# Selective scan: where GpSimd's seven drives take their B from

## What is computed

```python
xc = silu(conv(x_in) + conv_b)
sel = einsum('ble,se->bls', xc, sel_w)
Bm, Cm = sel[..., R:R+N], sel[..., R+N:]
dt = softplus(einsum('blr,er->ble', sel[..., :R], dt_w) + dt_b)
dA = exp(dt[..., None] * A)
dBu = dt[..., None] * Bm[:, :, None, :] * xc[..., None]
h = dA_t * h + dBu_t                    # the scan over t
y = einsum('ben,bn->be', h, C_t)        # summed over the 16 states
y = (y + D_param * xc) * silu(z)
```

## Time and profile before

| | us |
|---|---|
| median of 3 runs (1496.01 to 1501.19) | 1496.17 |
| the profiled execution | 1499.47 |
| its span, first to last instruction | 1497.7 |
| scan stage of the first pair, first scan's start to last GpSimd product's end (81.13 to 194.15) | 113.0 |
| busy in the span: PE, DVE, ACT, POOL | 1282.9, 1013.5, 592.0, 471.3 |

### The profile page before, as it was taken

How to read it: one execution, slowest core, us unless ns; L and a number is a source line. 1 busy time by engine, 2 the same in 40 slices (tenths; PEclk the granted TensorE clock), 3 DMA queues, 4 the chain that set the end, 5 groups by cost and what they waited for, 6 DMA issues and landing times.

```text
span 1497.7 us, 16634 instructions
## 1 busy us (share of the span) xinstructions
PE 1282.9 (86%) x5914; PEld 551.0 (37%) x5930; DVE 1013.5 (68%) x1106; ACT 592.0 (40%) x815; POOL 471.3 (31%) x254
## 2 busy tenths in 40 slices
PE   6957789989985789998997678999899687899988
PEld 2312333337422233334742223332573232333366
DVE  2589865575558895567555988556746599755683
ACT  0353443325344334333525433532451644343245
POOL 3259810012006990002200798000210199600030
PEclk9979999999997999999999899999999889999998
DMA  8234420000013442000001343200000134220000
GB/s 248 97 129 150 145 82 18 1 1 1 15 38 107 155 154 64 8 1 1 2 15 46 125 153 129 72 1 1 1 1 15 60 139 156 102 54 1 1 2 15
DMA packets 43378, 93.65 MB, mean 63 GB/s; under 512 B 6786, under 2 KB 23970, under 8 KB 42786
## 3 DMA queue, kind: packets, MB, share of 16 engines
q1 hardware_dynamic: 42690, 88.25, 17.8%
q10 hardware_dynamic: 608, 4.34, 1.0%
HBM read 87.84 MB, written 4.73 MB: 62 GB/s over the span
## 4 chain that ended last, share of the span: by engine, by line
PE 56%; DVE 14%; POOL 10%; ACT 8%; issue 7%; DMA 3%; SPq 1%; POOLq 0%; DVEq 0%; ACTq 0%
PE ps L654 8%; PE ps L667 8%; PE ps L675 7%; POOL scratch L456 6%; DVE scratch L1160 6%; PE ps L606 5%; PE ps L537 4%; PE ps L523 4%; DVE scratch L1149 3%; PE ps L770 2%; DVE scratch L1196 2%; PE ps L584 2%; PE ps L822 2%; PE ps L550 2%; DMA scratch<-c_rows 2%
## 5 line engine op out<-in xcount | busy, mean ns | idle before, releaser
L456 POOL TENSOR_TENSOR scratch<-scratch 128x1024 f32<-128x1024 f32 x124 | 291.2, 2367 | 340.1 <-DVE scratch L1160 340.0
L606 PE MATMUL ps<-scratch,consts 128*128 128x512 f32 x512 | 257.8, 637 | 15.4 <-POOL scratch L456 15.2
L470 POOL TENSOR_TENSOR scratch<-scratch,rmax 128x1024 f32<-128x1024 f32 x32 | 61.5, 1923 | 594.1 <-DVE rmax L1267 594.1
L1160 DVE TENSOR_TENSOR_SCAN scratch<-ps,scratch 128x1024 f32<-128x1024 f32 x100 | 225.5, 2278 | 0.5
L933 ACT ACTIVATE ps<-steps,vec 128x1024 f32<-128x1024 f32 x128 | 143.0, 1117 | 197.8 <-DVE scratch L1160 195.9
L1196 DVE TENSOR_TENSOR scratch<-scratch,ps 128x1024 f32<-128x1024 f32 x108 | 131.8, 1221 | 129.1 <-PE ps L667 122.6
L584 PE MATMUL ps<-bc,pick 128*128 128x512 bf16 x240 | 83.3, 427 | 125.4 <-DVE scratch L1149 80.7
L979 ACT ACTIVATE scratch<-ps 128x1024 f32<-128x1024 f32 x108 | 108.8, 1022 | 182.2 <-PE ps L654 182.2
L606 PEld LDWEIGHTS ps<-scratch,consts 128*128 128x128 f32 x512 | 101.9, 204 | 136.3 <-issue 92.8
L1149 DVE TENSOR_TENSOR scratch<-steps,ps 128x1024 f32<-128x1024 f32 x100 | 122.1, 1221 | 38.2 <-PE ps L584 31.9
L654 PE MATMUL ps<-h_odd,w 64*128 64x512 f32 x512 | 142.1, 641 | 3.8 <-ACT scratch L979 3.8
(11 more groups left out here) (197 smaller groups left out, 1590.0 us busy)
## 6 DMA issues: line engine op xcount, KB each, us to landing
scratch<-c_rows SPq DMA_DIRECT2D x128, 512.0 KB, 3.7
steps<-routed_table SPq DMA_DIRECT2D x128, 64.5 KB, 1.9
decayT<-in_decayT SPq DMA_DIRECT2D x8, 512.0 KB, 17.5
work<-in_table ACTq DMA_DIRECT2D x1, 2064.0 KB, 13.7
routed_table<-work SPq DMA_DIRECT2D x1, 2064.0 KB, 8.3
w<-in_w ACTq DMA_DIRECT2D x4, 512.0 KB, 20.2
out<-h_even SPq DMA_DIRECT2D x4, 512.0 KB, 2.6
bc<-in_x_next SPq DMA_DIRECT2D x3, 512.0 KB, 3.6
```

The costliest lines, as they stand in the source:

```text
L456: pool.tensor_tensor(hc_slot(k), hs_slot(k), c_slot(k), ALU.mult).then_inc(sem["hc_ready"], 1)
L606: m = mm(ps[:, 6 + c, :], ident, hc_slot(k)[:, c * CH:(c + 1) * CH], start=(n == 0), stop=(n == NS - 1))
L1160: dve.tensor_tensor_scan(hs_slot(k), banks(dA_bank(k)), dbu_slot(k), 0.0, ALU.mult, ALU.add).then_inc(sem["scanned"], 1)
```

## The change

For the seven GpSimd drives B no longer goes through TensorE, banks 0 and 1 and ScalarE. The DRAM tensor gets all 32 rows of B and C (`bc_rows`), so the two stores are twice as large, and SyncE reads B's row broadcast over the partitions into `b_sb`, ahead of the C row of step j-1, once the scan of the drive before has read `b_sb`. `copy_b`, `B_ORDER` and the seven spreads are gone; `DVE_DRIVES` lists the 25 steps that are left, and TensorE spreads the next of them at each of these steps. GpSimd's drive of step j moves from behind product j-4 to behind product j-3. The arithmetic is that of before, but that these seven steps take fp32 B in place of the sum of its three bf16 parts.

```diff
--- before.py
+++ after.py
@@ -45,9 +45,7 @@
 U_LATE = (7, 8, 11, 12)
 
 POOL_DRIVES = (5, 9, 13, 17, 21, 25, 29)
-B_ORDER = list(range(2 * NS))
-for _j in POOL_DRIVES:
-    B_ORDER[_j - 1:_j + 1] = [_j, _j - 1]
+DVE_DRIVES = [k for k in range(2 * NS) if k not in POOL_DRIVES]
 C_RING = 3
 
 Y_GATED = (NS + 8, NS + 11)
@@ -67,7 +65,7 @@
 
     xin_ps=NC, z_ps=NC, z_ready=2 * NC, xc_ready=2 * NC, sel_ps=2, dt_ps=2, sel_hi=2, sel_read=2, sel_split=1 + NC,
     dt_read=2, dt_exp=2, dt_ln=2, dt_ready=1, dt_late=NN, mid_late=1, u_ready=1, u_late=NN,
-    b_ps=2 * NS, dA_ready=2 * NS, dbu_ready=2 * NS - len(POOL_DRIVES), b_copied=len(POOL_DRIVES),
+    b_ps=2 * NS - len(POOL_DRIVES), dA_ready=2 * NS, dbu_ready=2 * NS - len(POOL_DRIVES), b_loaded=16 * len(POOL_DRIVES),
     dbu_pool=len(POOL_DRIVES), scanned=2 * NS, hc_ready=2 * NS - 1, hc_last=NC,
     c_rows=2, c_stored=16 * 2, c_loaded0=16 * 11, c_loaded1=16 * 11, c_loaded2=16 * 10,
     y_summed=2 * NS + 1, y_copied=1, gated_first=NC, gated_y=NC,
@@ -143,7 +141,7 @@
         av_bd = sb("av_bd", [P, P])
         fiT = sb("fiT", [P, 2, HID])
 
-        c_dram = nc.dram_tensor("c_rows", (2, NS, T), F32, kind="Internal").ap()
+        c_dram = nc.dram_tensor("bc_rows", (2, 2 * NS, T), F32, kind="Internal").ap()
         table_dram = nc.dram_tensor("routed_table", (P, LAYERS, NX, WCOL), F32, kind="Internal").ap()
         consts = sb("consts", [P, i["consts"].shape[1]])
         pick = sb("pick", [P, 2 * NS], BF16)
@@ -351,18 +349,25 @@
             sp.dma_start(table_dram, table).then_inc(sem["stored"], 16)
             def move(pair, more):
                 sp.wait_ge(sem["c_rows"], at(pair, "c_rows", 1))
-                sp.dma_start(c_dram[0], c_rows(0)[NS:2 * NS]).then_inc(sem["c_stored"], 16)
+                sp.dma_start(c_dram[0], c_rows(0)).then_inc(sem["c_stored"], 16)
                 sp.wait_ge(sem["c_stored"], at(pair, "c_stored", 16))
                 for k in range(2 * NS):
                     g, n = divmod(k, NS)
                     if k == C_RING:
                         sp.wait_ge(sem["c_rows"], at(pair, "c_rows", 2))
-                        sp.dma_start(c_dram[1], c_rows(1)[NS:2 * NS]).then_inc(sem["c_stored"], 16)
+                        sp.dma_start(c_dram[1], c_rows(1)).then_inc(sem["c_stored"], 16)
                     if k == NS:
                         sp.wait_ge(sem["c_stored"], at(pair, "c_stored", 32))
+                    if k + 1 in POOL_DRIVES:
+
+                        n_ = POOL_DRIVES.index(k + 1)
+                        if n_:
+                            sp.wait_ge(sem["scanned"], at(pair, "scanned", POOL_DRIVES[n_ - 1] + 1))
+                        g_, row = divmod(k + 1, NS)
+                        sp.dma_start(b_sb, c_dram[g_, row].partition_broadcast(P)).then_inc(sem["b_loaded"], 16)
                     if k >= C_RING:
                         sp.wait_ge(sem["hc_ready"], at(pair, "hc_ready", k - C_RING + 1))
-                    sp.dma_start(c_slot(k), c_dram[g, n].partition_broadcast(P))\
+                    sp.dma_start(c_slot(k), c_dram[g, NS + n].partition_broadcast(P))\
                       .then_inc(sem[f"c_loaded{k % C_RING}"], 16)
                 sp.wait_ge(sem["h_ready"], at(pair, "h_ready", NN))
                 sp.wait_ge(sem["stored"], 16)
@@ -454,13 +459,13 @@
                     if k >= 4:
                         pool.wait_ge(sem["y_summed"], at(pair, "y_summed", k - 3))
                     pool.tensor_tensor(hc_slot(k), hs_slot(k), c_slot(k), ALU.mult).then_inc(sem["hc_ready"], 1)
-                    if k + 4 in POOL_DRIVES:
-                        j = k + 4
+                    if k + 3 in POOL_DRIVES:
+                        j = k + 3
                         pool.wait_ge(sem["u_ready"], at(pair, "u_ready", 1))
                         if j >= NS:
                             pool.wait_ge(sem["u_late"], at(pair, "u_late", NN))
                         n_ = POOL_DRIVES.index(j) + 1
-                        pool.wait_ge(sem["b_copied"], at(pair, "b_copied", n_))
+                        pool.wait_ge(sem["b_loaded"], at(pair, "b_loaded", 16 * n_))
                         pool.tensor_tensor(b_sb, u[:, j // NS, :], b_sb, ALU.mult).then_inc(sem["dbu_pool"], 1)
 
                 for m in range(NM):
@@ -570,16 +575,13 @@
 
 
                 def spread_b(i):
-                    k = B_ORDER[i]
+
+                    k = DVE_DRIVES[i]
                     g, n = divmod(k, NS)
                     pe.wait_ge(sem["sel_split"], at(pair, "sel_split", 1 + NC * g))
                     pe.wait_ge(sem["dt_read"], at(pair, "dt_read", 1))
                     if i:
-                        last = B_ORDER[i - 1]
-                        if last in POOL_DRIVES:
-                            pe.wait_ge(sem["b_copied"], at(pair, "b_copied", POOL_DRIVES.index(last) + 1))
-                        else:
-                            pe.wait_ge(sem["dbu_ready"], at(pair, "dbu_ready", drives_up_to(last)))
+                        pe.wait_ge(sem["dbu_ready"], at(pair, "dbu_ready", i))
                     for c in range(NC):
                         m = mm(ps[:, c, :], pick[:, n:n + 1].to_broadcast([P, P]),
                                bc[:, g, c * CH:(c + 1) * CH], start=True, stop=True)
@@ -611,11 +613,8 @@
                 spread_b(0)
                 spread_b(1)
                 for k in range(2 * NS + LAG):
-                    if k + 2 in POOL_DRIVES:
-                        spread_b(k + 1)
-                        spread_b(k + 2)
-                    elif k and k + 1 < 2 * NS and k + 1 not in POOL_DRIVES:
-                        spread_b(k + 1)
+                    if k in DVE_DRIVES[1:-1]:
+                        spread_b(DVE_DRIVES.index(k) + 1)
                     if k == 2 * NS:
 
                         pe.wait_ge(sem["dbu_ready"], at(pair, "dbu_ready", PER["dbu_ready"]))
@@ -933,16 +932,6 @@
                     act.activation(banks(dA_bank(k)), dt[:, k // NS, :], ACT.Exp, scale=v("A", k % NS))\
                        .then_inc(sem["dA_ready"], 1)
 
-                def copy_b(j):
-                    act.wait_ge(sem["b_ps"], at(pair, "b_ps", B_ORDER.index(j) + 1))
-                    n_ = POOL_DRIVES.index(j)
-                    if n_:
-                        act.wait_ge(sem["scanned"], at(pair, "scanned", POOL_DRIVES[n_ - 1] + 1))
-                    else:
-                        act.wait_ge(sem["c_stored"], at(pair, "c_stored", 16))
-                    act.activation(b_sb, banks(0), ACT.Copy).then_inc(sem["b_copied"], 1)
-
-
                 first_parts(0)
                 dt_above(0)
                 dt_size(0)
@@ -967,8 +956,6 @@
                         act.wait_ge(sem["y_summed"], at(pair, "y_summed", NS))
                         act.wait_ge(sem["c_stored"], at(pair, "c_stored", 32))
                         act.activation(y_sum, banks(6), ACT.Copy).then_inc(sem["y_copied"], 1)
-                    if k + 2 in POOL_DRIVES:
-                        copy_b(k + 2)
                 norm(0)
 
 
@@ -1141,7 +1128,7 @@
                 def drive(k):
                     if k in POOL_DRIVES:
                         return
-                    dve.wait_ge(sem["b_ps"], at(pair, "b_ps", B_ORDER.index(k) + 1))
+                    dve.wait_ge(sem["b_ps"], at(pair, "b_ps", drives_up_to(k)))
                     if k >= 2:
                         dve.wait_ge(sem["scanned"], at(pair, "scanned", k - 1))
                     if k == NS:
```

## The result

The changed kernel took 1515.76 us (median of 1508.62, 1513.13, 1518.39 and 1522.39), the kernel before, run beside it, 1497.85. The ratio is 1.0117, 95% interval 1.0075 to 1.0159: slower by 17.9 us. The forecast was 1485.2, faster, with a range to 1495.

What follows compares the result with a forecast made beforehand. In the scan stage VectorE and GpSimd were taken as both nearly full, VectorE waiting 31.9 us for B's spreads. A gain of 23.0 less 12.0 for late B rows, 11.0 us, took 1496.17 to 1485.2; range 1473 to 1495.

Steps and rivals of the forecast that it cites:

- VectorE up to S(6): VectorE in the first pair: step 6's scan ends 26.32 us after step 0's scan starts.
- S(0): S(k) is step k's scan on VectorE; this is step 0's, from whose start each pair's times are counted.
- the cover of y's copy: ScalarE's copy of y and decay 19 end at 149.3, before step 19's scan is due at 149.9: covered by 0.6.
- where B is late: Drives 13, 17, 21, 25 and 29, where GpSimd runs without a gap, wait for B; 5 and 9 do not.
- GpSimd's work: GpSimd from step 6's product to step 30's, with drives 9 to 29: 80.5 us if it never waits.
- H(30): H(k) is step k's product on GpSimd; this is step 30's.
- how late B's row is: B lands 5.2 us after step j-5's product, asked for at 4.6: 0.6 late, twenty times, 12 us.
- the fourth case: Rival: B rows queue behind two C rows, 1.9 late, 38 us against 23: slower, 1511; chance 0.10.
- that H(30) sets the end of the stage: End of the scan stage: the last two matmul sums and the last gate follow GpSimd's product of step 30.
- the third case: Rival: B rows 0.8 to 1.4 late, or TensorE's lower clock costing 5.6 at y's copy; 1495; chance 0.20.
- the 23.0 without waits: Scan gain over four pairs if GpSimd never waits: 6.2, 6.7, 6.3 and 3.8 us.
- The sum: Whole forecast: 23.0 less 12.0 for late B rows is 11.0 us gained, 1485.2 against the median.

Runs made afterwards that it cites:

- x3: Changed kernel without the B rows, GpSimd's seven drives multiplying by xc instead: 1492.63 us, ratio 0.9876 to the kernel before.
- x17: Changed kernel, B's row ahead of C row j-2, zero matmuls (seven, five) behind the attention's first and third turns: 1482.51 us, ratio 0.9884.
- x2: Changed kernel with B's row issued ahead of the C row of step j-2, not j-1: 1481.25 us, ratio 0.9853 to the kernel before.
- x4: Changed kernel with eight zero matmuls ahead of the sum of each step behind a late GpSimd drive: 1502.00 us, ratio 1.0001.
- x1: Changed kernel once more with no edit: 1524.39 us, ratio 1.0104 to the kernel before.
- x18: Changed kernel with seven and five zero matmuls behind the attention's first and third turns: 1503.62 us, ratio 1.0020 to the kernel before.
- x19: Kernel before with seven and five zero matmuls behind the attention's first and third turns: 1497.04 us, ratio 0.9973.
- x15: Changed kernel with eight zero matmuls in the middle of each pair's expert stage: 1518.72 us, ratio 1.0146 to the kernel before.
- x13: Kernel before with eight zero matmuls in the middle of each pair's expert stage: 1515.87 us, ratio 1.0133.
- x9: Changed kernel with eight zero matmuls behind each of the attention's first three turns: 1514.94 us, ratio 1.0096 to the kernel before.
- x10: Kernel before with eight zero matmuls behind each of the attention's first three turns: 1515.54 us, ratio 1.0099.
- x11: Changed kernel, B's row ahead of C row j-2, eight zero matmuls behind each of the attention's first three turns: 1491.13 us, ratio 0.9936.
- x5: Kernel before with only GpSimd's drive moved from behind product j-4 to behind j-3: 1511.31 us, ratio 1.0037.
- x16: Changed kernel with B's row ahead of the C row of step j-2, run again, twelve runs: 1498.66 us, ratio 0.9889.

## Why the prediction was wrong

**Right: VectorE up to S(6).** It ended 26.34 us after S(0), 26.32 was said. **Right: the cover of y's copy, though all of it came later.** The copy started at 149.06 where the sum has 147.1, for two late rows cost 2.8 by then and not 1.2. Decay 19 behind it ended at 151.09 (149.3 was said), and S(19) started without a wait at 151.83 (149.9): a cover of 0.7 for the 0.6 that was said. **Right: where B is late.** In each pair drives 13, 17, 21, 25 and 29 waited, 5 and 9 did not, twenty waits in all. **Right, nearly: GpSimd's work.** The way from S(0) to H(30)'s end with no late row is 107.6 to 108.1 in x3, where 26.32 + 80.5 = 106.8 was said. Most of the difference is in waits of a product for its scan, as the 0.89 above. They are missing in my sum, although it called the two engines level: 3.9 us over four pairs.

**Wrong, the term that failed first: how late B's row is.** I said 0.6, from one pair of C rows of which the second landed 1.4 behind the first. Measured are 1.12 on the mean, 22.4 us and not 12. In the first pair these five B rows landed 2.5, 2.1, 1.6, 2.0 and 1.8 behind the C row issued 0.4 ahead of them, 2.0 on the mean. A C row of 3.6, and 2.0, and 0.1 for waking make 5.7 against the 4.6 that GpSimd leaves: the 1.1 of the trace. The line view of B's DMA:

```profile
DMA to landing us min/median/max: 4.5/5.0/5.9
```

The Trainium skill, SBUF — State Buffer, "The DMA setup-cost knee", has a DMA at 2 us plus its bytes over 436 GB/s. The estimate from it, 4.4 from the issue of the C row ahead, is below all five of the first pair, which took from 5.0 to 6.1; the measurement decides. Why the distance is 2.0 and not 1.4 wasn't separated: another C row, issued 1.9 later, was under way beside the B row, and the two C rows had one behind them too. That third row was issued 0.8 behind the first and not 0.6, so the fourth case should have read 2.1 late; it didn't come true either way.

**Wrong: that H(30) sets the end of the stage.** I let the last sums follow it unchanged. In x17 GpSimd's last four products run without a gap, and the gate comes 3.5 us behind H(30)'s end, not 2.9: TensorE's own run of sum, skip and twelve sums (1.98, 1.88, 5.31 above) starts when H(28) is there, and H(30) comes 0.5 earlier against it than before. That is 0.5 to 0.6 per pair, 2.2 us (tails of 13.9 in sum in x2, 11.7 before). Where TensorE had dropped to its lower level behind a late drive, the tail was 5.7, another 2.2; x4 took that away. I had the lower level in the third case, but at y's copy, where its cover held.

**The scan, summed.** Of the 23.0 without waits, 22.4 went to the rows, 1.2 to the rest of the way from S(0) to H(30)'s end (112.4 to 113.1 per pair, 23.6 in sum above the four times 106.8), 6.6 to the tails (18.3 against 11.7 in sum). That is -7.3, and the stages are 7.3 us longer. The 3.9 shrank to 1.2 because the waits don't add up: where rows are late, no product behind H(6) waits for its scan in this trace. The 7.3 is that of one execution: x1 lost 2.7 in the scan, x18 4.4 against x19, x15 14.0 against x13. The fourth case had the right sign with another mechanism. It wanted B behind two C rows and 1.15 us late, which didn't happen; with 1.2 to 3.9 and 2.2 gone elsewhere, the scan loses from (23.0 - 3.9 - 2.2) / 20, about 0.85, to 0.98 late. The profiled execution was forecast at 1488.5 and took 1518.39: of the 29.9 us, 18.3 are the scan's (7.3 lost for 11.0 won) and 11.6 lie in the attention behind the fourth scan.

**Wrong by leaving it out: the attention's clock.** The sum followed the scan alone and took what lies behind it as fixed. Filling its two gaps took 12.1 us off (x18 against the changed kernel), most of the 17.9. Of 89 runs of the kernel before 8 lay above 1504, of the changed one's eight all lay above 1508. The gaps of 2.02 and 1.62 are in both; with both filled, none of the 24 stretches in the traces of x9, x10, x11, x17, x18 and x19 has a long fall, so they are a condition of it. Why the changed kernel meets it so often stays open. The length of the scan is not it alone: x5 with a scan of 460.0 has a low clock in most runs, x2 and x16 with 445 in some, the kernel before with 462.0 in few. What x5 shares with the changed kernel is the move of the drive, but x2, x3 and x16 have that too; the kernel before has not.

The traces have one more sign. In each of its four stretches behind a scan the kernel before has TensorE at 0.50 for a short time some 8 us behind the gate, and in the changed kernel's fourth, the one that falls, it stays at 1.00. The windows of 4 us there, TensorE's columns alone, before and then changed (clock third from the end):

```profile
1308.00:1312.00 4.00, 4.00 (x9) 0.57 0.29 66
```

```profile
1315.00:1319.00 4.00, 4.00 (x15) 1.00 0.27 66
```

In the eight traces without matmuls by zero in the attention or the expert stage (the two kernels, x1 to x5 and x16), 14 of the 32 stretches have this early drop. They are some 2 us longer (252.2 for 250.5), and none of them has a long fall, one of 17 us or more; of the 18 without it 6 have one. So the kernel before enters the attention differently. Whether that protects it no run tests.

## What to carry to other kernels

A load that replaces a copy has to be issued by the clock of the one who asks for it: count from what SyncE waits for to the moment the tile is asked for, and give the landing the longest row of that DMA, not the median, or one whole step more, as moving it ahead of the C row did here (-24 us in the scan). Before you price the end of a wait, ask what else holds its engine: with 21.7 us of GpSimd's waits gone, the scans of x5 were 2.0 us shorter. Where two engines are level and a third is close behind, work out the gain by each of the three chains and take the smallest. And look for short gaps of TensorE in the stages behind an edit too: a dozen matmuls by zero per pair, in two gaps of 2.0 and 1.6 us, cost nothing that could be measured and took 12 us off.

## What the runs showed of the hardware

The same instructions with the same two gaps ahead of them ran on at the upper level in one execution and 24 us at 0.50 in another, which costs a pair 8 to 13 us (260.7 against 252.2 in x4, 209.4 behind x3's fourth scan against 196.0 behind x2's). Twelve runs of one kernel spread over 41 us (x16), with a mean granted clock of 0.95 and above in the five up to 1480.3 and 0.93 to 0.94 in the others; ten with the gaps filled spread over 7 (x18), at 0.937 to 0.944, so the mean clock tells runs of one kernel apart and not kernels. Of two 512 KB rows issued one behind the other, 0.4 us apart, the second landed 1.6 to 2.5 us behind the first (the five late B rows of the changed kernel's first pair).
